# A four-layer vision tower on one core: gates moved from the experts' outputs to their hidden units, second products with 512 columns

## The reference

```python
h = h + _L0_ffn_ref(_layernorm(h), ...)   # 8 experts, 256 hidden units, relu, one expert per token
h = h + _L1_ffn_ref(_layernorm(h), ...)   # 8 experts,  64 hidden units, gelu, two experts per token
h = h + _L2_ffn_ref(_layernorm(h), ...)   # 8 experts, 128 hidden units, gelu, two experts, a norm after
h = h + _L3_ffn_ref(_layernorm(h), ...)   # 4 experts, 128 hidden units, gelu, after a graph attention
# each of them amounts to
for e in range(E):
    out += gate[:, e:e+1] * (act(x @ W1[e] + b1[e]) @ W2[e] + b2[e])
```

## Time and profile before

| | |
|---|---|
| median of three runs | 14245.91 us |
| the profiled execution's own time | 14248.64 us |
| its span (first to last instruction) | 14246.8 us |
| mean granted TensorE clock | 0.716 |
| PE busy | 8506.4 us, 60% |
| DVE busy | 6583.8 us, 46% |
| POOL busy | 6318.2 us, 44% |
| ACT busy | 3350.6 us, 24% |
| DMA engines busy (slice by slice) | 0.0 to 0.2 |

### The profile page before, as it was taken

How to read it: one execution, slowest core, us unless ns; L and a number is a source line. 1 busy time by engine, 2 the same in 40 slices (tenths; PEclk the granted TensorE clock), 3 DMA queues, 4 the chain that set the end, 5 groups by cost and what they waited for, 6 DMA issues and landing times. The chain is left out here.

```text
span 14246.8 us, 157338 instructions
## 1 busy us (share of the span) xinstructions
PE 8506.4 (60%) x62435; PEld 5418.0 (38%) x62435; DVE 6583.8 (46%) x9074; ACT 3350.6 (24%) x5899; POOL 6318.2 (44%) x6565
## 2 busy tenths in 40 slices
PE   6997798588899967987777774749520000000006
PEld 4775575366667735652222222536310000000004
DVE  5778376200007862139999994452421111111123
ACT  2443343244344432222222221222100000000001
POOL 0005577767710002646666663000036666666640
PEclk8997888788989875559999996555555555555555
DMA  2000000000000000000000001000001111111100
GB/s 102 9 11 18 12 12 11 19 12 20 11 25 9 12 18 10 1 1 2 2 2 2 2 2 1 1 0 0 0 10 19 19 19 17 19 19 19 17 12 7
DMA packets 290069, 178.08 MB, mean 12 GB/s; under 512 B 226797, under 2 KB 274957, under 8 KB 284752
## 3 DMA queue, kind: packets, MB, share of 16 engines
q0 software_dynamic: 209952, 32.71, 3.9%
q1 hardware_dynamic: 79472, 136.16, 3.0%
HBM read 116.87 MB, written 51.56 MB: 12 GB/s over the span
## 5 line engine op out<-in xcount | busy, mean ns | idle before, releaser
L2010 POOL DMA_INDIRECT sorted<-by_row_rows,by_row_idx x2112 | 2031.1, 962 | 2650.9 <-PE bank L1219 1729.1
L2097 POOL DMA_INDIRECT sorted<-r_rows,r_pos x2112 | 2049.9, 971 | 1926.3 <-PE bank L566 1284.5
L2229 POOL DMA_INDIRECT g_g<-table,g_idx x2112 | 2024.7, 959 | 643.6 <-issue 643.6
L1722 DVE TENSOR_TENSOR a_top<-bank,a_k 128x2048 f32<-128x2048 f32 x1024 | 2254.0, 2278 | 6.3 <-ACT a_k L1758 3.8
L2331 PE MATMUL bank<-sc_ident,g_tails 128*20 128x128 f32 x99 | 18.2, 307 | 3136.7 <-PEq L65 3134.9
L1884 PE MATMUL bank<-a_top,sc_pick_row 128*32 128x512 f32 x8192 | 1105.0, 620 | 515.5 <-DVE a_top L1722 492.6
L2331 PEld LDWEIGHTS bank<-sc_ident,g_tails 128*20 128x20 f32 x99 | 7.1, 98 | 3147.6 <-issue 3135.0
L2250 DVE CAST g_nodef<-g_es 128x64 f32<-128x64 int32 x33 | 6.4, 195 | 2492.9 <-DMA g_ep<-sorted 2492.9
L762 DVE TENSOR_TENSOR f_qa<-f_qa,bank 128x512 f32<-128x512 f32 x128 | 82.2, 684 | 2318.6 <-PE bank L556 1982.7
L547 PE MATMUL bank<-f_space,f_proj 128*128 128x512 f32 x2048 | 978.5, 601 | 199.7 <-issue 160.5
L1219 PEld LDWEIGHTS bank<-sw_e_w,e_hid 128*128 128x128 f32 (+1 forms) x4608 | 893.1, 329 | 363.6 <-issue 293.4
(11 more groups left out here) (467 smaller groups left out, 13013.8 us busy)
## 6 DMA issues: line engine op xcount, KB each, us to landing
f_stage<-folded SPq DMA_DIRECT2D x16, 2304.0 KB
sorted<-r_rows,r_pos POOLq DMA_INDIRECT x2112, 2.1
sorted<-by_row_rows,by_row_idx POOLq DMA_INDIRECT x2112, 2.1
g_g<-table,g_idx POOLq DMA_INDIRECT x2112, 2.6
states<-g_st SPq DMA_DIRECT2D x33, 768.0 KB
fp_raw<-t_modes SPq DMA_DIRECT2D x4, 2304.0 KB, 15.0
folded<-fp_turned SPq DMA_DIRECT2D x4, 2304.0 KB, 7.8
f_bb<-t_features SPq DMA_DIRECT2D x4, 2048.0 KB, 11.4
```

The lines of the kernel that those rows point to most:

```text
L1722: v.tensor_tensor(top[:, n % RD].rearrange("p q (h s) -> p q h s", s=S), q, kk, ALU.max).then_inc(top_done, 1)
L2010: p.indirect_dma_start(out=self.dst, out_offset=bass.IndirectOffsetOnAxis(ap=self.idx[:, k:k + 1], axis=0), in_=self.rows[:, k, :], in_off ...
L2097: p.indirect_dma_start(out=self.dst, out_offset=bass.IndirectOffsetOnAxis(ap=self.pos[:, k // PART_STEPS, at:at + 1], axis=0), in_=self.ro ...
L2229: p.indirect_dma_start(out=g[:, k_in, j, :], out_offset=None, in_=d["table"], in_offset=bass.IndirectOffsetOnAxis(ap=idx[:, k_in, j:j + 1] ...
```

## The change

It has these parts:

1. A unit is 128 hidden rows (`units` per group: 16 in e0, 4 in e1, 8 in e2, 4 in e3). `first` is one product of 64 rows per unit.
2. `spread` is new: a product with 8 rows (4 in e3) of a constant (`pick`) as weights and the transposed gates as 512 columns, which writes one expert's gates onto all 128 rows of a PSUM bank. It is needed once per expert (`shared` is 2 in e0, so one per two units; in e1 `pick_pairs` covers the two experts of a unit; elsewhere one per unit).
3. DVE (`gate_unit`) multiplies each unit's `hid` by that bank; `gather`, `start_acc` and their sums are gone.
4. `second` has `w2` as weights (128 rows, 64 columns wide) and streams `hid`, 512 columns, summed in PSUM over all experts in two halves of a bank. The product of `b2` and the gates opens the sum.
5. ACT (`move_out`) copies the group's 128x512 sum to `yt`; `turn_out` transposes it and adds the halves by four products with `fold`; DVE (`take_out`) puts it into `acc`. `turn_gates` now shares PSUM bank 7 with `turn_out` and waits for `take_out`.
6. 320 of the second scatter's sends are in e0 instead of 448: 128 while the tokens are transposed, and the others paced over the loop. l1 attention has 28 sends a tile.
7. In `fno` the rows of column scatters are loaded in four parts of 528 columns, and three buffers share memory. Three small weights more are loaded (`fold`, `pick`, `pick_pairs`).

```diff
@@ fno, SyncE @@
-                def rows(k):
-                    if k >= 2:
-                        sp.wait_ge(sent[(k - 2) % HD_SENDS], 16 * STEP_COLS * ((k - 2) // HD_SENDS + 1))
-                    sp.dma_start(ranks.rows[:, k % 2], ranks.edges[:, k * STEP_COLS:(k + 1) * STEP_COLS, :]).then_inc(rows_in[k % 2], 16)
+                def rows(part):
+                    if part >= 2:
+                        done = PART_STEPS * (part - 1)
+                        for j in range(HD_SENDS):
+                            sp.wait_ge(sent[j], 16 * STEP_COLS * len(range(j, done, HD_SENDS)))
+                    sp.dma_start(ranks.rows[:, part % 2], ranks.edges[:, part * QC:(part + 1) * QC, :]).then_inc(rows_in[part % 2], 16)
...
@@ experts @@
-    wide = 2 * pair // per
-    steps = E // wide
+    units = E * F // P
+    shared = max(1, F // P)
...
-        h_bank, y_bank, b_bank, gt_bank, l_bank = t.bank[0:4], t.bank[4:6], t.bank[6], t.bank[7], t.bank[2]
+        h_bank, g_bank, y_bank, o_bank, l_bank = t.bank[0:3], t.bank[3:5], t.bank[5:7], t.bank[7], t.bank[2]
...
-                        p.wait_ge(y_done, n + 1)
+                        if n < 2 * GS:
+                            p.wait_ge(xt_moved, n // 2 + 1)
+                        else:
+                            p.wait_ge(y_done, (n - 2 * GS) * GS * units // (rounds - 2 * GS) + 1)
...
                 def turn_gates(g):
+                    if g >= 2:
+                        pe.wait_ge(o_used, g - 1)
...
+                def first(n):
+                    g, u = n // units, n % units
+                    if n >= 3:
+                        pe.wait_ge(u_moved, n - 2)
+                    half = slice(u % 2 * D, u % 2 * D + D)
+                    pe.matmul(h_bank[n % 3][:, :], w1[half, u // 2, :], xt[half, g * 512:(g + 1) * 512], start=True, stop=True).then_inc(u_done, 1)
+
+                def spread(m):
+                    g, v = m // (units // shared), m % (units // shared)
+                    if v == 0:
+                        pe.wait_ge(gt_moved, g + 1)
+                    if m >= 2:
+                        pe.wait_ge(gated, shared * (m - 1))
+                    pe.matmul(g_bank[m % 2][:, :], pick[0:E, v, :], gate_t[0:E, g % 2, :], start=True, stop=True).then_inc(g_spread, 1)
+
+                def second(n):
+                    g, u = n // units, n % units
+                    if u == 0:
+                        if g >= 2:
+                            pe.wait_ge(y_moved, g - 1)
+                        pe.matmul(y_bank[g % 2][0:D, :], b2[0:E, :], gate_t[0:E, g % 2, :], start=True, stop=False, skip_group_check=True)
+                    pe.wait_ge(gated, n + 1)
+                    half = slice(u % 2 * D, u % 2 * D + D)
+                    pe.matmul(y_bank[g % 2][half, :], w2[:, u, :], hid[:, n % HR, :], start=(u == 1), stop=(u >= units - 2), skip_group_check=True).then_inc(y_done, 1)
+
+                def turn_out(g):
+                    pe.wait_ge(y_moved, g + 1)
+                    pe.wait_ge(gt_moved, min(g + 2, GS))
                     if g >= 1:
+                        pe.wait_ge(o_used, g)
                     for k in range(GT):
+                        last = pe.matmul(o_bank[:, k * D:(k + 1) * D], yt[:, g % 2, k * P:(k + 1) * P], t.fold[:, :], start=True, stop=True)
+                    last.then_inc(o_done, 1)
...
+                for n in range(GS * units):
+                    g, u = n // units, n % units
+                    if n + 2 < GS * units:
+                        first(n + 2)
+                    if (n + 1) % shared == 0 and (n + 1) // shared < GS * units // shared:
+                        spread((n + 1) // shared)
                     second(n)
+                    if u == 2 and g >= 1:
+                        turn_out(g - 1)
+                        if g + 1 < GS:
+                            turn_gates(g + 1)
+                turn_out(GS - 1)
...
+                for n in range(GS * units):
+                    g, s = n // units, n % units
+                    if n == 2:
+                        turned_gates(1)
+                    if s == 2 and g >= 1:
+                        move_out(g - 1)
+                    if s == 3 and 1 <= g < GS - 1:
+                        turned_gates(g + 1)
...
+                def gate_unit(n):
+                    v.wait_ge(u_moved, n + 1)
+                    v.wait_ge(g_spread, n // shared + 1)
+                    v.tensor_tensor(hid[:, n % HR, :], hid[:, n % HR, :], g_bank[n // shared % 2][:, :], ALU.mult).then_inc(gated, 1)
...
-TILE_SENDS = 26
-FIRST_SENDS = 448
+TILE_SENDS = 28
+FIRST_SENDS = 320
```

More of the change, by code:

```diff
@@ L413, in _ @@
                             group_in(u // LAYERS + 1)
-                        for k in range(SEND_STEPS - 2):
-                            if (send_at(k) + 4) // 8 == n:
-                                rows(k + 2)
-                                if k % PART_STEPS == 1:
-                                    place_part(k // PART_STEPS)
+                        for part in range(PARTS):
+                            if n == send_at(PART_STEPS * part + 1) // 8:
+                                place_part(part)
+                            if part >= 2 and n == send_at(PART_STEPS * part - 5) // 8:
+                                rows(part)
                         if n == ROW_CHUNK:
@@ L1112, in tensor, with experts @@
         pass
-def experts(t, name, make_gate, E, F, act_fn, w1, b1, w2, b2, base, finish, gain=None, shift=None, beside=None):
+def experts(t, name, make_gate, E, F, act_fn, w1, b1, w2, b2, pick, base, finish, gain=None, shift=None, beside=None):
     nc = t.nc
     CK, GS = TILES // IT, TILES // GT
-    per = max(1, F // P)
-    pair = max(1, P // F)
-    wide = 2 * pair // per
-    steps = E // wide
+    units = E * F // P
+    shared = max(1, F // P)
     HR = 6
-    half = P // pair
     with ExitStack() as ctx:
@@ L1183, in turn_gates @@
                 def turn_gates(g):
+                    if g >= 2:
+                        pe.wait_ge(o_used, g - 1)
+                    for k in range(GT):
+                        last = pe.transpose(o_bank[0:E, k * P:(k + 1) * P], gates[:, g * GT + k, :], t.ident[:, :])
+                    last.then_inc(gt_turned, 1)
+                def first(n):
[4 more added lines that the diff above has]
+                    pe.matmul(h_bank[n % 3][:, :], w1[half, u // 2, :], xt[half, g * 512:(g + 1) * 512], start=True, stop=True).then_inc(u_done, 1)
@@ L1198, in first @@
-                def first(n):
-                    g, s = n // steps, n % steps
-                    if n >= 2:
-                        pe.wait_ge(u_moved, 2 * n - 2)
-                    for a in range(2):
-                        r = slice(a * D, (a + 1) * D)
-                        pe.matmul(h_bank[(2 * n + a) % 4][:, :], w1[r, s, :], xt[r, g * 512:(g + 1) * 512], start=True, stop=True).then_inc(u_done, 1)
-                def second(n):
-                    s = n % steps
-                    pe.wait_ge(u_moved, 2 * n + 2)
-                    yr = 1 if pair > 1 else 2
-                    if n >= yr:
-                        pe.wait_ge(y_used, n - yr + 1)
-                    for k in range(GT):
-                        for w in range(wide):
-                            for j in range(per):
-                                a = w // pair if pair > 1 else (j if per > 1 else w)
-                                q = w % pair
-                                r = slice(q * half, (q + 1) * half)
-                                col = (w // pair if pair > 1 else w) * GT * D + k * D
-                                last = pe.matmul(y_of(n, q)[:, col:col + D], hid[r, (2 * n + a) % HR, k * P:(k + 1) * P], w2[r, 2 * s + a, :],
-                                                 start=(j == 0), stop=(j == per - 1))
-                    last.then_inc(y_done, 1)
@@ L1268, in _, with turned_gates @@
                 gate.scalar(act)
[L1269 to L1283 removed]
+                def turned_gates(g):
+                    act.wait_ge(gt_turned, g + 1)
+                    if g >= 2:
+                        act.wait_ge(y_done, (g - 1) * units)
+                    act.activation(gate_t[0:E, g % 2, :], o_bank[0:E, :], ACT.Copy).then_inc(gt_moved, 1)
@@ new lines, in move_out @@
+                def move_out(g):
+                    act.wait_ge(y_done, (g + 1) * units)
+                    if g >= 2:
+                        act.wait_ge(o_done, g - 1)
+                    act.activation(yt[:, g % 2, :], y_bank[g % 2][:, :], ACT.Copy).then_inc(y_moved, 1)
+                turned_gates(0)
+                for n in range(GS * units):
[6 more added lines that the diff above has]
+                        turned_gates(g + 1)
+                    act.wait_ge(u_done, n + 1)
+                    if n >= HR:
+                        act.wait_ge(y_done, n - HR + 1)
+                    act.activation(hid[:, n % HR, :], h_bank[n % 3][:, :], act_fn, bias=b1[:, s:s + 1]).then_inc(u_moved, 1)
```

(19 more changed lines are left out.)

119 lines of the change are left out of this document (35 added, 84 removed).

## The result

The changed kernel takes 15230.3 us (median of four runs, 15225.3 to 15237.4); the kernel before, measured with it, 14246.4. The ratio is 1.069 (95% interval 1.0672 to 1.0709): 6.9% slower. The forecast was 15,630 us with a range of 14,930 to 15,740, so the direction and the range held, and the size, 984 us for a forecast of 1384, was 400 us off.

A forecast was written before the change was run, and what follows sets the result against it. PE at the lower clock was taken to bound the expert loops: 14248.6 + 1409 - 25 = 15,632.6, less 2.7 to the runs' median, gives 15,630 us. Range 14,930 to 15,740; the forecast's own 15,500 to 15,700.

The forecast's parts named there:

- The lower clock in the expert loops: All four expert loops: PE stays at granted clock 0.50, judged likelier because of few-row products; loops sum to +1409 us.
- The prices at that clock: PE in the expert loops: first and spread 2.01 us each, second 1.89, 5.4 per group; e0 group 83.9.
- the wait for take_out: PE before each group's transposes waits for DVE's copy and hand-overs: 0.7 us, bounds 0.42 and 1.5.
- the 25 us that I took off for a start at the upper clock: Start of each expert loop: first units can keep the upper clock, 6 us off per loop, 25 in all.
- The two sends more per tile hidden in l1 attention: POOL in l1 attention: two more sends end before the next tile's start; 0, bounds 0 and 64 x 1 us.
- the ACT and DVE work of the expert layers hidden under PE: Expert loops: ACT's longest stretch some 2.5 us under 4.0 of PE; DVE's 351 us of gate products cost nothing.
- Loading rows of column scatters in four parts: fno: the four-part loads lie under a PE without idle time; 0 us, bounds 0 and +7.
- The side-by-side rival: Expert loops: a spread runs beside the preceding first on rows 64 to 127; 515 us less, 15,115; chance 0.07.
- The rival of a full clock: All four expert loops at the upper clock level; total 14,240 us, or 14,190; chance 0.11, half of it faster.
- a mixed clock: Expert loops: clock changes between levels, up in long units, down at groups' small products; 14,935 us; chance 0.13.

The follow-up runs named there:

- e0: Not a run: an expert layer, 16 units per group; its stage took 886.3 us in the kernel before and 1439.5 in the changed kernel.
- e1: As a run, not the layer: kernel before with part 7 alone (four-part row loads, shared buffers), slower chip: 16,990 us against 17,006, ratio 0.9996.
- e2: Here an expert layer (stage 518.0 us before, 920.8 after); as a run: changed kernel with fno's old row loads, slower chip, 18,645 us, ratio 1.097.
- e3: As a run, not the layer: kernel before with part 7, each part loaded by 12 DMAs of 44 columns issued together; slower chip: 17,003 us, ratio 1.0002.
- e6: Changed kernel with every first product over 128 rows and only the first two spreads of each layer issued (values differ): 13514.8 us, one run.
- e8: Changed kernel with every first product over 128 rows in place of 64, all spreads kept (values differ): 13918.6 us, one run.
- e9: Changed kernel with 64-row first products kept and only the first two spreads of each layer issued: 14488.0 us, one run.
- e10: Changed kernel reordered, same output: two units' first products side by side, and their second products too: 13567.0 us, ratio 0.9522 to the kernel before.
- e11: As e10, but the two spreads per pair meant to stand apart in layers e1 to e3, gates transposed earlier; slower chip: 17,032 us against 17,012, ratio 1.0016.
- e4: Kernel before with part 7, SyncE also waiting at the 46 old places for scatters with nothing to load behind; slower chip: 16,994 us, ratio 0.9993.
- e12: Same kernel as run e3, measured again, also on the slower chip: 17,042 us in one run against 17,012 of the kernel before.

## Why the prediction was right, and what of it was wrong

1. The lower clock in the expert loops: right. All four are at 0.50, and e6, e8 and e9 show what decides: with 128-row first products and nothing else changed the clock goes up (0.98 in e0, 0.88 to 0.91 elsewhere), without the spreads it does not. The reason given in the prediction was products of few rows, with the weight on the 8-row spreads; in this order it is the first products of 64 rows that decide, and the spreads cost the rest of the clock in e1 to e3. So the step was right with a cause only half named.
2. The prices at that clock: right. First and spread 2.00 (2.01), second 1.90 (1.89), a group of e0 83.78 us (83.9). turn_out 1.97 (1.89), the wait for take_out 0.57 (0.7). Every layer came out 6 to 8 us below the forecast without the 25 us that I took off for a start at the upper clock; with it the sum is 9 us off. In e0 no such start shows: its first pair of firsts already took 2.02 us (5152.24 to 5154.26).
3. The two sends more per tile hidden in l1 attention, and the ACT and DVE work of the expert layers hidden under PE: right. l1 attention takes 2334.0 against 2332.6 us, and the layers come out at PE's prices.
4. The step that failed: "Loading rows of column scatters in four parts lies under fno, where PE has no idle time (200.00 of 200) and POOL is half idle [...] 0, bounds 0 and +7". The window from 860 to 1060 lies ahead of the first scatter. Behind it PE waited: in fno it was busy 4387 of 5102 us, after the change 4380 of 4713. The change looked like one of size, 48 loads into four; what it removed was 46 waits of SyncE for GpSimd's scatters (2735.2 us), with the loads of projections, weights and features and the writes of the tokens behind them. Only two of the four loads have such a wait, and SyncE's queue shows none of length there. This term measured -389 to -392 us, and lay outside the bounds that I had given it, below nothing. The bound had no reason that excluded a gain; the prediction counted the loads and not what was queued behind their waits.
5. The side-by-side rival fell as priced: a spread starts 2.00 us after the first ahead of it. The rival of a full clock fell too, but it was one edit away: e8 has it, with e0 at 0.98, and its expert layers come out 73 us longer than before where the rival had them 5 us shorter.

The range would have held the expert layers alone as well (14,246 + 1375 = 15,621). That it also held with fno's 389 us off is luck: it reached down to 14,930 for rivals of another kind (a mixed clock, spreads side by side), and the narrower range given for the forecast itself, 15,500 to 15,700, missed. The two halves of the change had opposite signs, and the prediction had only one.

## What to carry to other kernels

When a load on a shared queue carries a wait, list what is queued behind it and who needs that; measure the waits of the issuing queue over the whole stage before calling a load hidden, and never from one clean window. A product that uses half of the array's rows can cost twice: once by its own time and once by the clock of everything around it, as the 64-row firsts did here. Read the granted clock of each loop, and test what raises it before counting products. With products paired in rows and in columns, the same idea as in this change took 292 us off the expert layers in place of adding 1375; with the 393 us of fno the kernel is 4.8% faster instead of 6.9% slower.

## What the runs showed of the hardware

The step from 64 to 128 rows in one product of each unit, at the same number of columns, brought the granted clock of e0's loop from 0.50 to 0.98, and took a first product from 2.00 to 1.06 us (changed kernel and e8). One spread of 8 rows per unit went with 0.89 in e1's loop where no spreads went with 1.00 (e8 and e6).

Two 128-row products whose weights are 64 columns wide and whose results go to different halves of a PSUM bank run side by side: two cost 1.01 us (e10), one 1.00 (e8).

On one chip the kernel before takes 17,006 us in place of 14,246. There e1, e2 and e3 are as long as on the others (331.7, 521.2 and 306.6 us with the old expert layers); fno is 6604 to 6638 us and l1 attention 3529 to 3704. ACT's waits in fno on that chip (e11's run), with "remote" for a releaser that the trace doesn't show, are these:

```profile
ACT f_space L674 <- remote: 1315.3, 84, 40.8
ACT f_space L668 <- remote: 434.3, 33, 44.2
```

They come while GpSimd scatters, on several engines: DVE's in fno are 2322.0 us in 25 (e1's run). But scatters alone don't bring them: e0 with the old expert layers is 886 to 893 us long on that chip (e1, e3, e4, e12) against 886.3, with 448 sends beside it. What causes them stays open.
